# Tanh gates folded into weights and biases, biases added on TensorE, and a new order of work in a five-stage transformer pipeline

## What is computed

```python
x = x + jnp.tanh(g_xattn[0]) * _L0_xattn_ref(_layernorm(x), ctx_768, Wq, Wk, Wv, Wo, bo)      # 4 heads
x = x + jnp.tanh(g_ffn[0])   * _L0_ffn_ref(_layernorm(x), W, b, lora_down, lora_up, down_aux, up_aux)
x = x + jnp.tanh(g_xattn[1]) * _L1_xattn_ref(_layernorm(x), ctx_768, ctx_768, Wq, bq, Wk, bk, Wv, bv)  # 1 head
x = x + jnp.tanh(g_ffn[1])   * _L1_ffn_ref(_layernorm(x), W_qkv, b_qkv, W_gate, b_gate, W_experts, b_experts)
```

## Time and profile before

| | |
|---|---|
| median of 3 runs | 963.12 us (962.2 to 964.64) |
| the profiled execution's own time | 963.9 us |
| its span in the profile | 962.1 us |
| PE busy | 842.9 us (88% of the span) |
| DVE busy | 821.5 us (85%) |
| ACT busy | 562.4 us (58%) |
| POOL busy | 505.0 us (52%) |
| granted TensorE clock, mean | 0.977 |

### The profile page before, as it was taken

How to read it: one execution, slowest core, us unless ns; L and a number is a source line. 1 busy time by engine, 2 the same in 40 slices (tenths; PEclk the granted TensorE clock), 3 DMA queues, 4 the chain that set the end, 5 groups by cost and what they waited for, 6 DMA issues and landing times. The chain is left out here.

```text
span 962.1 us, 34570 instructions
## 1 busy us (share of the span) xinstructions
PE 842.9 (88%) x11700; PEld 663.7 (69%) x11700; DVE 821.5 (85%) x1979; ACT 562.4 (58%) x1230; POOL 505.0 (52%) x692
## 2 busy tenths in 40 slices
PE   5578898999999999999999999999999999998875
PEld 2457776777777767777776777777677777776653
DVE  4678899888989988898998888999988898999664
ACT  2444666655666666656666665666665566666443
POOL 4122665454566555556665555566545456655443
PEclk9787999999999999999999999999999999999998
DMA  8211122121112221111122121112212111211100
GB/s 302 67 56 46 51 69 68 51 67 53 44 56 65 67 64 55 60 49 53 58 67 67 51 66 51 48 53 67 67 51 67 54 44 56 65 51 48 37 6 11
DMA packets 37298, 58.49 MB, mean 61 GB/s; under 512 B 5644, under 2 KB 23938, under 8 KB 37140
## 3 DMA queue, kind: packets, MB, share of 16 engines
q1 hardware_dynamic: 37268, 58.10, 18.9%
HBM read 34.44 MB, written 3.67 MB: 40 GB/s over the span
## 5 line engine op out<-in xcount | busy, mean ns | idle before, releaser
L1275 POOL TENSOR_TENSOR acc<-part,acc 112x256 f32<-112x256 f32 x256 | 269.9, 1054 | 38.9 <-DVE acc L1150 20.2
L1246 POOL TENSOR_SCALAR ln_ve<-ln_mv 112x1 f32<-112x1 f32 x128 | 32.4, 253 | 203.5 <-DVE ln_mv L963 203.5
L813 ACT ACTIVATE part<-bankE,cgS 112x256 f32<-112x256 f32 x256 | 107.7, 476 | 32.9 <-DVE cgS L1113 22.5
L1258 POOL TENSOR_TENSOR xg<-xin,gbrow 112x256 f32<-112x256 f32 x32 | 25.2, 787 | 187.3 <-DVE x L1022 187.3
L323 PE MATMUL bankE<-wexs_hi,xT_hi 128*112 128x512 f16 x256 | 99.9, 390 | 16.3 <-ACT part L813 16.3
L1058 DVE TENSOR_TENSOR p_lo<-p2T,p_hi 112x896 f16<-112x896 f32 x64 | 95.2, 1526 | 9.4 <-ACT p_hi L804 9.4
L323 PE MATMUL bankE<-wexs_hi,xT_lo 128*112 128x512 f16 x256 | 96.9, 379 | 0.0
L323 PE MATMUL bankE<-wexs_lo,xT_hi 128*112 128x512 f16 x256 | 96.9, 379 | 0.0
L1250 POOL TENSOR_TENSOR ln_rs<-ln_ve,cst 112x1 f32<-112x1 f32 x128 | 72.8, 569 | 10.7
L796 ACT ACTIVATE p2T<-quad 112x896 f32<-112x896 f32 x64 | 55.3, 915 | 22.2 <-PE quad L571 22.2
L1120 DVE TENSOR_REDUCE mx<-quad 112x8 f32<-112x896 f32 x64 | 66.8, 1086 | 1.2 <-issue 0.2
(11 more groups left out here) (237 smaller groups left out, 3341.3 us busy)
## 6 DMA issues: line engine op xcount, KB each, us to landing
ctf<-in_ctx_T SPq DMA_DIRECT2D x32, 375.0 KB, 3.0
ctn<-in_ctx_n SPq DMA_DIRECT2D x32, 375.0 KB
kvB<-kvA SPq DMA_DIRECT2D x32, 281.2 KB, 2.4
kc<-kvB SPq DMA_DIRECT2D x32, 187.5 KB
xin<-in_x SPq DMA_DIRECT2D x32, 112.0 KB, 2.0
out_x<-xout SPq DMA_DIRECT2D x32, 112.0 KB, 2.2
wex<-in_w_exp SPq DMA_DIRECT2D x1, 2048.0 KB, 9.9
kcA<-kvB SPq DMA_DIRECT2D x32, 46.9 KB
```

The costliest lines, as they stand in the source:

```text
L813: act.activation(part[:, e, :], bankE[0:LQ, n * D:(n + 1) * D], ACT.Identity, scale=cgS[:, e:e + 1])\
L1275: pool.tensor_tensor(acc[:], part[:, 2 * j + n, :], acc[:], ALU.add).then_inc(moe_sum[j].sem, 1)
```

## The change

The four gates no longer scale activations. POOL multiplies them once into weights and biases: `gate_wo`, `gate_wf`, `gate_wv`, `gate_wvg` and `gate_b_lin`. The biases of the output projection and of the linear map become a further product, of a tile of ones with a packed bias (`b_o`, `b_f`), in `project_o` and `ffn0`; that of the second cross attention sits in a row of its value weights. `add_bias`, `gate_scales` and the two gate products in `recip1` and `norm2` go. As `xin` is freed by `normalise(0)`, the sequence is loaded a second time, as `x0`, for the first residual. The memsets of the four probability buffers `p_hi` and `p_lo` clear only their padding columns. The order of every engine's list is new: some steps are split (`max2`, `combine_copy`, `norm0`, `norm2`, `qk_lo`, `gate_negmax`), some swapped, and the border between iterations lies elsewhere.

```diff
-        gsc = sb("gsc", [LQ, 6])
-        brow = sb("brow", [LQ, 3, D])
-        gbrow = sb("gbrow", [LQ, 3, D])
...
+            def load_x0(b):
+                if past(b - 1):
+                    sp.wait_ge(ln[1].sem, ln[1].after("stats", b - 1))
+                sp.dma_start(x0[:], x[b]).then_inc(x0_in.sem, DMA)
...
                 if A and more: load_ctx_T(a + 1)
+                if EE: store(e)
+                if B: load_x0(b)
                 if B: copy_B_to_C(b)
                 if A: copy_A_to_B(a)
                 if A: load_weights(a)
-                if EE: store(e)
...
-                    oT_hi[:, c, :], oT_lo[:, c, :], lin_hi[:, WO, c, :], lin_lo[:, WO, c, :])]).then_inc(wo_s.sem, 1)
+                    oT_hi[:, c, :], oT_lo[:, c, :], lin_hi[:, WO, c, :], lin_lo[:, WO, c, :])] + [(ones16, b_o)]).then_inc(wo_s.sem, 1)
...
-                    h[:, c, :], l[:, c, :], lin_hi[:, WF, c, :], lin_lo[:, WF, c, :])]).then_inc(f0_s.sem, 1)
+                    h[:, c, :], l[:, c, :], lin_hi[:, WF, c, :], lin_lo[:, WF, c, :])] + [(ones16, b_f)]).then_inc(f0_s.sem, 1)
...
-                if B: norm_T(0, b, bankB, wo_s, "x1", b - 1)
-                if EE: experts(1, e)
-                if DD: out1(d)
-                if EE: max2_T(e)
-                if B: project_q(b)
-                if EE: scores2_T(e)
+                if EE: experts(1, e)
+                if EE: max2_T(e)
+                if B: layer1_A(b)
+                if DD: out1(d)
+                if B: norm_T(0, b, bankB, wo_s, "x1", b - 1)
+                if EE: scores2_T(e)
+                if B: project_q(b)
...
-                dve.wait_ge(o1_s.sem, o1_s.after("recip", c))
-                ts(gr1[:], rr1[:], gsc[:, 2:3], None, ALU.mult).then_inc(o1_s.sem, 1)
...
-                ts(rec2[:], rec2[:], gsc[:, 4:5], None, ALU.mult).then_inc(pv2.sem, 1)
-                dve.wait_ge(pv2.sem, pv2.after("gated", d))
...
-            pool.memset(p2_hi[:], 0.0).then_inc(filled, 1)
-            pool.memset(p2_lo[:], 0.0).then_inc(filled, 1)
+            pool.memset(p2_hi[:].rearrange("p n i q -> p (n i) q")[:, :, LQ:P], 0.0).then_inc(filled, 1)
+            pool.memset(p2_lo[:].rearrange("p n i q -> p (n i) q")[:, :, LQ:P], 0.0).then_inc(filled, 1)
...
-            def add_bias(dst, src, n, ch, b, ready, step, free, fstep):
-                pool.wait_ge(ready.sem, ready.after(step, b))
...
-                pool.tensor_tensor(dst[:], src[:], gbrow[:, n, :], ALU.add).then_inc(ch.sem, 1)
+            def gate_wo(a):
+                if first(a):
+                    pool.wait_ge(linear_in, 2 * DMA)
+                    pool.wait_ge(gates_s.sem, gates_s.after("tanh", 0))
+                    pool.tensor_scalar(lin[:, WO], lin[:, WO], th[:, 0:1], None, ALU.mult).then_inc(gated_s.sem, 1)
```

More of the change, by code:

```diff
@@ L173, in flamingo_kernel @@
         filled = sem("filled")
-        gates_s = chain("gates_s", "tanh scales rows")
+        gates_s = chain("gates_s", "tanh")
+        gated_s = chain("gated_s", "wo b_lin wf wv wvg b_vg")
+        blin_s = chain("blin_s", "scaled half packed")
         lora_s = chain("lora_s", "ps1 t1 ps2 t2 ps added")
@@ L274, in store @@
                 sp.dma_start(out[d], xout[:]).then_inc(stored.sem, DMA)
[L276 to L277 removed]
+            sp.dma_start(gate_in[:], gates).then_inc(gates_in, DMA)
             load_ctx_T(0)
@@ L509, in out1 @@
                 if first(c_):
-                    pe.wait_ge(layer1_in, 4 * DMA)
+                    pe.wait_ge(gated_s.sem, gated_s.after("wv", 0))
                 pe.wait_ge(zs.sem, zs.after("copy", c_))
@@ L820, in body @@
                 A, B, C, DD, EE = (v is not None for v in (a, b, c, d, e))
+                if C: probs0_hi(0, c)
+                if A: wkv_hi(a)
+                if C: exp0(1, c)
+                if C: A_hi_copy(c)
+                if C: probs0_hi(1, c)
+                if C: wf_hi(c)
+                if EE: xT_hi(3, e, bankD, moe[NG - 1], "ps")
+                if DD: xT_hi(2, d, bankC, qps, "ps")
                 if B: keys_hi(b)
@@ new lines, in body @@
+                if EE: start_sum(e)
+                if C: residual(wo_s, "x1", c, x1, bankB, x0, f0_s, "x2", 1)
+                if B: normalise(0, xin, b)
+                if C: stats(1, x1, wo_s, "x1", c)
+                if DD: wex_lo_half(0, d)
+                if A: wkv_lo(a)
+                if B: lora_add(b)
+                if EE: wex_lo_half(3, e)
+                if C: mean_var(1, c)
+                if DD: recip1(d)
+                if B: xT_lo(0, b, bankB, qs, "ps")
+                if DD: residual(o1_s, "x3", d, x3, bankC, x2, acc_s, "sum", 3)
@@ L1176, in body @@
+                if DD: stats(3, x3, o1_s, "x3", d)
                 if C: normalise(1, x1, c)
-                if A: wkv_lo(a)
-                if DD: bias_experts(d)
-                if DD: stats(3, x3, o1_s, "x3", d)
-                if B: lo(qs, b, q_lo[:], cols(bankB, KD, LQ), 1 / SW, q_hi[:], st0[1], "ps", b - 1)
                 if DD: mean_var(3, d)
                 if A: ctxT_lo(0, a)
-                if C: xT_lo(1, c, bankC, f0_s, "ps")
+                if B: lo(qs, b, q_lo[:], cols(bankB, KD, LQ), 1 / SW, q_hi[:], st0[1], "ps", b - 1)
```

284 lines of the change are left out of this document (149 added, 135 removed).

## The result

The changed kernel takes 922.94 us (median of 4 runs, 919.31 to 923.47) where the kernel before takes 963.88 (4 runs beside them, 962.2 to 964.67). The ratio is 0.957, with a 95% interval of 0.954 to 0.960; 922 was predicted. The profiled execution took 923.47 us, its span is 921.5.

The account below looks back on a forecast made before the run. The bound was a loop of 21.5 us on DVE and 6.35 on PE. Terms sum to -1.4 us, period 26.5; 27 gaps give -37, start -1, drain -3: 923 profiled, 922 for the median, range 903 to 946.

Parts of the forecast that it names:

- `gr` and `norm2`'s product: On DVE's part of the loop: removing the product `gr` saves 0.41 us and removing the gate product in `norm2` 0.27 us per iteration.
- The wait for `rstd(1)`: DVE's `xn` behind `x3` waits for POOL's `rstd(1)`; a further step now covers this, saving 0.14 us per iteration.
- Waits of DVE for its own results: Dependent DVE steps (`comb`, `cgS`, `x1`, two `cT`) get other steps between them: -0.7 us per iteration, bounds 0 and 0.7.
- DVE and POOL: DVE and POOL steps hinder each other; the new order avoids 0.9 of 1.5 us lost per iteration, bounds 0 and -1.5.
- `normalise(0)` moved in: `normalise(0)` moves from behind the stage-C `xn`, where it cost nothing, into DVE's 21.5 us stretch: +0.34 us per iteration.
- New waits: New DVE waits per iteration: `xT_lo` of stage B +0.4 us, `q_lo` and `max0` behind `exp2` +0.2, context copy +0.1.
- Bias products: PE's two added products of 256 columns, about 0.1 us each, lie inside its 2.2 us slack: 0; without slack, 0.2.
- SP's order: The sequence's second load and the store stand ahead of the copies on SP; claimed cost 0.
- Start: Kernel start: shorter memsets, but PE's start moves from 12.83 to about 15 us; net -1 us, bounds +3 and -5.
- Drain: Last four iterations: the same removed products save about 0.7 us each, -3 us together, without the POOL term.
- Rival 3: Slower: two POOL additions ahead of `rstd(1)` delay DVE's `xn`; at 2.0 us wait, period 28.5, kernel 979; chance 0.07.
- Rival 2: All DVE meetings with POOL go and waits are small: period perhaps 25.6, limited by PE, about 901 us; chance 0.10.

## Why the prediction was right

The time was right within 1 us, and the period too (26.45 for 26.5), but that the sum came out is luck: two of its terms were wrong by 0.8 us each, in opposite directions. Step by step, from start to start of DVE's instructions, against the 21 common iterations of before:

- **`gr` and `norm2`'s product**, -0.41 and -0.27: as forecast. **The wait for `rstd(1)`**, forecast -0.14: `x3` to the next step went from 0.62 to 0.60 only, since the statistics stand there now and need `x3` itself. -0.02.
- **Waits of DVE for its own results**, forecast -0.7 with 0.7 as the far bound: -1.48 between `max1` and `acc` (8.04 before, 6.16 now, and 0.40 of the difference is `x1`, which has moved behind `acc`). Gap by gap: the border at `rsg` 0.53, the one ahead of `x1` 0.43, `pick` to `comb` 0.22, `cgb` to `cgS` 0.20, `topf` moved out 0.07; the pair of `cT`, for which the forecast had 0.1, nothing. So the bound left out the largest gap of all. It also counted bare idle time, while a stalled step further loses the 0.08 us by which it would have overlapped its predecessor (`rsg` starts 0.07 behind a `comb` of 0.16). The experiments show the border and 0.29 of the gate steps. The gap ahead of `x1` was not tried by itself, and its cause stays open.
- **DVE and POOL**, forecast -0.9: about -0.1, the near bound ("as many additions meet as many steps"). The pair of `p_lo` became free (-1.02). But `add_experts(0)`, which starts at `acc`, now meets the stage-B `xn` (+0.39), the next pair meets `kvA` (+0.32), and the stage-C `xn` (+0.15) and the second `kvA` (+0.06) are longer. The stage-C `xn` was to become free and did not; that of stage DD was bare before, in 21 of 24 iterations. The sentence "DVE's steps there read PSUM, except one `xn`" had the first of the new meetings and gave it no price. That the lock is still in the loop is shown by the run with small additions, 0.83 us of period.
- **`normalise(0)` moved in**: +0.34, as forecast.
- **New waits**, forecast +0.7: +0.94, in other places, less 0.25 for a wait of DVE for ACT ahead of `xT_lo<-bankC` that is gone. `xT_lo<-bankB` +0.21 for 0.4; `q_lo` and `max0` nothing for 0.2; the context copy +0.50 for 0.1; and `rstd(2)` ahead of the stage-C `xn` +0.23, not foreseen. For the context copy both readings were off: the slack of 0.9 us is that of the earlier trace rows, and in the 21 common iterations POOL's `kvA` took 0.65 and ended 0.45 ahead of DVE's. DVE could come 1.4 us sooner behind `max1` now (10.35 without the 0.61 of waiting, for 11.79), POOL's result came only 0.5 sooner. DVE is so early mostly because the term of own results was twice its forecast.
- Small changes of `x1`, `x2` and others, -0.1. Sum -1.4, as forecast.
- **Bias products**, 0: the period is the same without them. **SP's order**, 0: the loads go out long before the copies.
- **Start**, forecast -1: PE's first key product at 14.38 (about 15 forecast), and -3.7 in all, within the bounds. What shortened the fill was not traced, and its size is uncertain: in profiled executions of the kernels with the border moved and with one more statistics instruction, the first `xout` came at 104.5 and at 107.6 or 108.7. The memsets, which I had named as what held ACT, are not what the first key product waits for afterwards.
- **Drain**, forecast -3: -0.3 in this execution. The granted clock (a mean of stretches at the two levels, 1.2 and 2.4 GHz, as a share of the higher) goes with it, by these windows of the last stretch, after (the first) and with the border moved (the second; its drain has the same work):

```profile
895.80:918.51 22.71, 15.89 (x168) 10.74 (x168) 9.86 (x26) 8.86 (x20) 7.45 (x10) 0.77 0.02 6
```

```profile
893.40:914.80 21.40, 13.59 (x168) 9.46 (x166) 9.86 (x26) 8.87 (x20) 7.49 (x10) 0.88 0.03 7
```

DVE, ACT and POOL are busy for the same time in both; PE is 2.3 us longer at a clock of 0.77, and the gap 1.3 longer. Over the last two gaps the difference is 2.8 us. Four further executions with the same drain, but for a bias product or the order of the gate steps, fall on the same two values: 46.5 and 46.7 us for the two gaps at clocks of 0.86 and 0.77 or 0.78, 43.7 and 43.8 at 0.89 and 0.88. Why the clock differs between them stays open. In the kernel before the same two gaps stood at 0.96 and 0.92. With the second kernel's gaps the drain is 94.5 us, and its gain, with the 5.4 us of phase taken off, 2.9: the forecast.

Of what the prediction said would show it, the period, `p_lo` below 1.4, `xT_lo<-bankB` waiting 0.25 and `max1` waiting about 0.5 came true. The stage-DD `xn` is at 0.41, as it mostly was before; the stage-C `xn` is at 0.91 and not at 0.41. `x3` starts right behind `xT_lo`. One sign of being wrong is there too: the stage-C `xn` starts 0.03 us behind the end of POOL's `ln_rs`, after 0.14 idle, in the median of the loop. Rival 3's mechanism exists: the run with POOL's other order is slower than the kernel before. It acts through `rstd(2)` behind a pile of additions, not through `rstd(1)`. Rival 2's ceiling, a period of 25.6 with PE full, is where the run with small additions ended.

The Trainium skill, page "SBUF — State Buffer", section "Who interferes with whom", describes the port pair that VectorE and GpSimd share as a lock held by one of them at a time. The run with small additions agrees: with less of POOL's work beside it `kvA` falls from 1.09 to 0.56 us, and `mx<-quad`, which reads PSUM, stays at 1.08 to 1.09 throughout. The lock works in the other direction too: POOL's `kvA` of 0.52 us took 0.64 where DVE's `xn` ran beside it.

## What to carry to other kernels

A step taken off the loop gives its time only as far as the next wait: here folding the gates alone gave 4 us, the order alone 27 and both 41, and the next 12 lay in a queue of DMA issues for which VectorE had not had to wait before. So when a stretch gets shorter, list every wait inside it with its slack, and shorten the first that runs out. A loop border, and small steps that wait for each other, belong behind a long instruction of the same engine; and when two engines hold each other off, compare the sum of lengths over bare lengths for every step they can meet, not only for the one that is slow now. Do it over many iterations: two with the same period can have their meetings in different places, and here the one that was read closely was of the rarer kind.

## What the runs showed of the hardware

- A loop border on VectorE takes about 0.46 us of idle time behind two steps of 0.16 us, and none where an instruction of 0.81 us stands ahead of these two (`rsg` to the next step: 0.62 against 0.11 start to start). In written-out iterations of the kernel before, the same pair of steps is 0.07 to 0.08 us apart.
- Moving two additions on GpSimd, with no work added, cost 1.74 us per iteration (26.45 to 28.19).
- Three steps of VectorE that need each other's results, back to back, cost 0.29 us more than with other steps between them, about 0.1 each.
- Five small copies on the SyncE queue took 0.49 to 0.83 us each to issue; one fewer brought the transfer behind them forward by 0.48 us (7.71 to 7.23 behind `max1`) and the period down by 0.45.
- TensorE's granted clock in the last stretch of the drain was 0.77, 0.88 and 0.92 in different executions; in the steady part it was 1.00.
